# Cross attention with one head: context rows made from the turned context on TensorE instead of loaded a second time

## The chip, the cores and the metric

One program on one core of a Trainium2 chip. The metric is the device time of one launch in microseconds (us); times are medians of several runs. The profile is one further execution, recorded by the hardware profiler.

## The reference, cut to what matters

The program is a two-layer network over 32 batches of 32 query rows of width 512, with a context of 257 rows of width 512 for each batch. The change touches the first block only, a cross attention with a single head:

```python
q   = layernorm(x) @ Wq + bq                 # 32 x 32 x 512
k   = ctx @ Wk + bk                          # 32 x 257 x 512
v   = ctx @ Wv + bv
sim = einsum('bid,bjd->bij', q, k) * 512**-0.5
x   = x + einsum('bij,bjd->bid', softmax(sim), v)
```

Self-attention, a layer of experts, a second cross attention, a second self-attention and a second layer of experts follow. They are the same before and after.

## The kernel before, in words

The kernel folds the key weights into the queries, so that the scores are products of a query tile with the context itself, and it applies the value weights after the weighted sum over context rows. So each context tile is needed twice: turned (width on the partitions, `ct`, loaded from `ctxT`) for the scores, and in natural rows (context rows on the partitions, `cn`, loaded from `ctx`) for the product of the probabilities with the context. Both are loaded from HBM, all in 32-bit floats. The 257th row of each batch is held apart (`cl`, loaded from `ctxLast`).

The 1024 query rows form 8 tiles of 128 rows (`NT`), and a tile spans 4 batches (`SEQ`). For one tile the loads are 4 pieces of `ctxT` with 514 KB, 4 pieces of `ctx` with 512 KB, and one of 8 KB for the last rows. `ct`, `cn` and the small tiles exist twice, picked by `u`, the tile's parity.

The function is `cross_one_head` (L313). Two blocks prepare it: the first (L363) folds the weights and loads tile 0, the second (L513) makes the queries and loads tile 1. The third block (L567) is the stage of this text. Each engine has a program of its own, in the order in which it is written, and the engines are tied by counting semaphores. What TensorE does for a tile `n`:

- `scores` (L699 to L707): the query tile with `ct`, 16 products in 32 instructions, 257 columns each, into bank `u`.
- `turn_p` (L709): three transposes of the probabilities into bank `2 + u`.
- `p_ctx` (L717): the last row and then `cn`, into bank `4 + u`.
- `turn_a` (L734): four transposes of the weighted sum into bank 6.
- `values` (L742): 12 products with the value weights, through the helper `mm3` (L128 to L130), into bank 7.

Before its loop TensorE does `scores` of tiles 0 and 1, `turn_p` and `p_ctx` of tile 0. The loop has three turns of two steps each, so six steps; step `n` (1 to 6) is

```python
scores(n + 1, u, i + 1)
turn_p(n, 1 - u)
turn_a(n - 1, u)
p_ctx(n, 1 - u, i + u)
values(n - 1, u)
```

and a tail finishes tiles 6 and 7. ScalarE copies the query tile (`q_tile`, L597), takes the exponentials (`exps`, L601) and copies the high part of the turned sum (`a_high`, L606). VectorE finds the maximum (`softmax_top`, L631), scales the last column (`last_p`, L640), copies the turned probabilities out (`keep_p`, L644 to L646), takes the low part (`a_low`, L650), scales the sum (`keep_a`, L656) and adds to `x` (`add`, L660, L661). The SP queue loads tile `n + 2`: the turned pieces (`load_turned`) once `scores` of tile `n` are done, the natural rows (`load_rows`) once `p_ctx` of tile `n` is done.

Of the kernel before, what the change touches and what calls it, by code (L numbers as in the profile page):

```python
# [19 lines left out]
ALU = mybir.AluOpType  # L20
# [3 lines left out]
P = 128  # L24
# [17 lines left out]
LEAD = 2  # L42
# [47 lines left out]
def build(nc, d, out):  # L90
    with ExitStack() as ctx:
# [221 lines left out]
        def cross_one_head():  # L313
# [12 lines left out]
            xn = [n_area.take(D) for _ in range(4)]  # L326
            root = n_area.take(NT)
            s_ctxT = [[sem(f"xa_ctxT{u}{j}") for j in range(SEQ)] for u in range(2)]
            s_ctx = [[sem(f"xa_ctx{u}{j}") for j in range(SEQ)] for u in range(2)]
            s_cl = [sem(f"xa_last_rows{u}") for u in range(2)]  # L330
            s_sc, s_pv = sem("xa_scores"), sem("xa_pv")
            s_x, s_id, s_b, s_wq, s_wk, s_wv = (
# [11 lines left out]
                for j in range(SEQ):  # L344
                    eng.dma_start(ct[u][j], d["ctxT"][SEQ * n + j]).then_inc(s_ctxT[u][j], 16)

            def load_rows(eng, n, u):
                eng.dma_start(cl[u][0:SEQ, :], d["ctxLast"][bass.ds(SEQ * n, SEQ), :]).then_inc(s_cl[u], 16)
                for j in range(SEQ):
                    eng.dma_start(cn[u][j], d["ctx"][SEQ * n + j, 0:2 * P, :]  # L350
                                  .rearrange("(k p) e -> p k e", p=P)).then_inc(s_ctx[u][j], 16)

            jobs = [(h, c) for h in range(NHALF) for c in range(DC)]
            L, MB = 4, 4
# [4 lines left out]
            with nc.sbuf_tensor("ra_fold", [P, R_FOLD], F32R) as ra2:  # L359
# [3 lines left out]
                with nc.Block() as block:  # L363
                    @block.sync
                    def _(eng):
                        eng.dma_start(staging[0], columns(d["L0_xattn_WqT"])).then_inc(s_wq, 16)
                        eng.dma_start(staging[1], columns(d["L0_xattn_WkT"])).then_inc(s_wk, 16)
                        eng.dma_start(x[:], d["x"].rearrange("(t p) d -> p t d", p=P)).then_inc(s_x, 16)
                        eng.dma_start(staging[2], columns(d["L0_xattn_Wv"])).then_inc(s_wv, 16)
                        load_turned(eng, 0, 0)  # L370
                        eng.wait_ge(s_ql, 1)
                        eng.wait_ge(s_kl, 1)
                        load_rows(eng, 0, 0)
                        eng.wait_ge(s_x, 16)
                        eng.wait_ge(s_b, 48)

# [132 lines left out]
            with nc.sbuf_tensor("fa_cross", [P, F_CROSS], F32) as fa2:  # L509
# [3 lines left out]
                with nc.Block() as block:  # L513
                    @block.sync
                    def _(eng):
                        load_turned(eng, 1, 1)
                        load_rows(eng, 1, 1)

                    @block.vector
                    def _(eng):  # L520
                        links = Links(eng, s_links1)
                        eng.wait_ge(s_tk, 1)
                        links.link(dve.reduce_sum(through_k, banks[:, MB + 3, 0:2 * DC].rearrange("p (c k) -> p c k", k=2), AX_X))
                        for j, (h, c) in enumerate(jobs):
                            eng.wait_ge(s_mm, j + 1)
                            dve.tensor_scalar(qp[:, c, h * HALF:(h + 1) * HALF], banks[:, MB + j % 4, :], through_k[:, c:c + 1],
                                              None, ALU.add).then_inc(s_out, 1)
                            if j == 0:
                                eng.wait_ge(s_urk, 1)
                            links.link(dve.scalar_tensor_tensor(away, x[:, j, :], moments[:, j, 0:1], u_row, ALU.subtract,  # L530
                                                                ALU.mult))
                            links.link(dve.reduce_sum(shift[:, j:j + 1], away, AX_X))
                        links.link(dve.tensor_tensor(shift, shift, rstd[:], ALU.mult))
                        dve.tensor_scalar(shift, shift, both[:, 0:1], None, ALU.add)


                    @block.tensor
                    def _(eng):
                        for j, (h, c) in enumerate(jobs):
                            cols, tok = slice(c * P, (c + 1) * P), slice(h * HALF, (h + 1) * HALF)  # L540
                            if c == 0:
# [18 lines left out]
                a = [f.take(D) for _ in range(2)]  # L560
                mx, top, bias, rs, rinv = (f.take(2) for _ in range(5))
                s_passed, s_own, s_last = (sem(f"xa_{n}") for n in ("passed", "own", "p_last"))
                (s_qg, s_bias, s_exp, s_tp, s_pt, s_a, s_at, s_ah, s_al, s_o, s_xa, s_links) = (
                    sem(f"xa_{n}") for n in ("q_tile", "bias", "exp", "p_turned", "p_kept", "a_kept",
                                             "a_turned", "a_high", "a_low", "out", "x_added", "links"))

                with nc.Block() as block:  # L567
                    @block.sync
                    def _(eng):
                        gain_loads(eng)  # L570
                        with eng.Fori(0, NT // 2 - 1) as i:
                            for u in range(2):
                                n = 2 * i + u

                                eng.wait_ge(s_sc, SEQ * n + 3 * SEQ)
                                load_turned(eng, n + 2, u)

                                eng.wait_ge(s_pv, SEQ * n + 2 * SEQ)
                                load_rows(eng, n + 2, u)

                    @block.gpsimd
                    def _(eng):
# [10 lines left out]
                    def _(eng):  # L593
# [10 lines left out]
                        def a_high(n, u):  # L604
                            eng.wait_ge(s_at, n + 1)
                            act.activation(at[u][0], chunks(banks[:, 6, :]), ACT.Copy).then_inc(s_ah, 1)  # L606

                        eng.sem_inc(s_exp, LEAD)
                        q_tile(0, 0)
                        q_tile(1, 1)  # L610
                        exps(0, 0)
                        exps(1, 1)
                        with act.Fori(0, NT // 2 - 1) as i:
                            for u in range(2):
                                q_tile(2 * i + u + 2, u)
                                exps(2 * i + u + 2, u)
                                a_high(2 * i + u, u)
                        a_high(NT - 2, 0)
                        a_high(NT - 1, 1)

                    @block.vector
                    def _(eng):
# [19 lines left out]
                        def keep_p(n, u):  # L642
                            eng.wait_ge(s_tp, n + 1)
                            dve.reciprocal(rinv[:, u:u + 1], rs[:, u:u + 1])  # L644
                            dve.tensor_copy(pt[u][:, 0:2, :], banks[:, 2 + u, 0:2 * P].rearrange("p (k t) -> p k t", k=2))
                            dve.tensor_copy(pt[u][0:SEQ, 2, :], banks[0:SEQ, 2 + u, 2 * P:3 * P]).then_inc(s_pt, 1)  # L646

                        def a_low(n, u):
                            eng.wait_ge(s_ah, n + 1)
# [3 lines left out]
                        def keep_a(n, u):  # L653

                            eng.wait_ge(s_pv, SEQ * n + 2 * SEQ)
                            dve.tensor_scalar(a[u], banks[:, 4 + u, :], rinv[:, u:u + 1], None, ALU.mult).then_inc(s_a, 1)  # L656

                        def add(n, u):
                            eng.wait_ge(s_o, n + 1)
# [32 lines left out]
                    def _(eng):  # L692
# [16 lines left out]
                        def turn_p(n, u):  # L709
                            eng.wait_ge(s_last, n + 1)  # L710

                            eng.wait_ge(s_pt, n + 1)
                            for k in range(2):
                                pe.transpose(banks[:, 2 + u, k * P:(k + 1) * P], pr[u][:, k * P:(k + 1) * P], ident[:])
                            pe.transpose(banks[0:SEQ, 2 + u, 2 * P:3 * P], last[u], ident[:]).then_inc(s_tp, 1)

                        def p_ctx(n, u, i):  # L717
                            eng.wait_ge(s_pt, n + 1 + LEAD)

                            eng.wait_ge(s_a, n + 1)  # L720

                            eng.wait_ge(s_cl[u], 16 * i + 16)
                            for j in range(SEQ):
                                eng.wait_ge(s_ctx[u][j], 16 * i + 16)
                            pe.matmul(banks[:, 4 + u, :], pt[u][0:SEQ, 2, :], cl[u][0:SEQ, :], start=True, stop=False)
                            for k in range(2):
                                for j in range(SEQ):
                                    ins = pe.matmul(banks[NQ * j:NQ * j + NQ, 4 + u, :],
                                                    pt[u][:, k, NQ * j:NQ * j + NQ], cn[u][j][:, k, :],
                                                    start=False, stop=k == 1)  # L730
                                    if k == 1:
# [17 lines left out]
                            ins.then_inc(s_o, 1)  # L749

                        scores(0, 0, 0)
                        scores(1, 1, 0)
                        turn_p(0, 0)
                        p_ctx(0, 0, 0)
                        with pe.Fori(0, NT // 2 - 1) as i:
                            for u in range(2):
                                n = 2 * i + u + 1
                                scores(n + 1, u, i + 1)
                                turn_p(n, 1 - u)
                                turn_a(n - 1, u)  # L760
                                p_ctx(n, 1 - u, i + u)
                                values(n - 1, u)
                        turn_p(NT - 1, 1)
                        turn_a(NT - 2, 0)
# [1561 lines left out]
def layouts(i):  # L2326
# [4 lines left out]
    def units(up1, up2, down):  # L2331
# [8 lines left out]
    ctx = i["ctx_1024"]  # L2340
    a = {
        "x": i["x"].reshape(T, D),
        "ctx": ctx,
        "ctxT": t(ctx).reshape(B, DC, P, S).transpose(0, 2, 1, 3),
        "ctxLast": ctx[:, S - 1, :],
        "ctxLastT": ctx[:, S - 1, :].T.reshape(DC, P, B).transpose(1, 0, 2),
# [40 lines left out]
```

## Time and profile before

| | us |
|---|---|
| median of 3 timed runs | 2224.11 (2219.28 to 2225.76) |
| span of the profiled execution, first to last instruction | 2252.5 |
| the stage of this text in it (third block) | 71.8 to 171.7 |
| its six loop steps | 83.9 to 152.4 |

The profiled execution has no other time than its span: what lies around the first and the last instruction isn't given for it. The median belongs to runs without the profiler. Times within the profile count from the span's start. PE is TensorE, PEld its weight loads, DVE is VectorE, ACT ScalarE, SP the queue that issues the loads; PEclk is the granted TensorE clock as a share of its full 2.4 GHz, so that 0.50 is 1.2 GHz.

### The profile page before, as it was taken

The numbers are of one execution on the slowest core, as the hardware profiler recorded it, in microseconds if no ns is written. First come the engines' busy times: TensorE is split into PE (matmuls) and PEld (weight loads), VectorE is DVE, ScalarE is ACT, GpSimd is POOL, SyncE is SP. The second block draws the span as 40 slices with busy tenths as digits, with TensorE's granted clock in tenths as the row PEclk, the third lists the DMA queues.
The fourth block names the chain that finished last, engine by engine and source line by source line (L and its number), as shares of the span: only waits on it lengthen the run. The fifth ranks groups of instructions, "written<-read, shape, count | busy, mean of one in ns | idle before, by whom it ended". The sixth has DMA issues, their size and how long they took to land. (4 is left out here: it accounts for less than half of the span.)

```text
span 2252.5 us, 44598 instructions
## 1 busy us (share of the span) xinstructions
PE 1805.6 (80%) x15646; PEld 1506.8 (67%) x15646; DVE 911.5 (40%) x2100; ACT 615.9 (27%) x1360; POOL 794.1 (35%) x540
## 2 busy tenths in 40 slices
PE   6776898735888884289999999968772799999993
PEld 5445676524777773278888888856552688888883
DVE  5445434463333331623333333335455433333333
ACT  2112433412222220223333333334343211111110
POOL 0004331124468305223333333313103299766302
PEclk8997999867999996699999999976796899999997
DMA  6562010175556325211111111010007355443203
GB/s 247 220 240 80 20 57 1 41 302 211 167 194 210 116 71 154 91 42 39 29 37 37 28 37 28 20 43 6 25 1 287 144 179 180 147 141 124 70 20 122
DMA packets 97195, 237.09 MB, mean 105 GB/s; under 512 B 9712, under 2 KB 26736, under 8 KB 97040
## 3 DMA queue, kind: packets, MB, share of 16 engines
q1 hardware_dynamic: 68768, 172.84, 22.1%
q10 hardware_dynamic: 20592, 36.98, 5.0%
q0 software_dynamic: 7680, 25.17, 3.3%
q8 instruction: 102, 1.67, 0.3%
q14 instruction: 53, 0.43, 0.1%
HBM read 183.58 MB, written 51.38 MB: 104 GB/s over the span
## 5 line engine op out<-in xcount | busy, mean ns | idle before, releaser
L128 PE MATMUL banks<-ra_DE 128*128 128x258 f32 (+2 forms) x912 | 321.0, 353 | 30.5 <-ACT fa_DE L2058 8.4
L128 PE MATMUL banks<-weights_F,rest_r_F 128*128 x920 | 304.5, 331 | 15.3 <-DVE rest_r_F L1752 11.2
L129 PE MATMUL banks<-ra_DE 128*128 128x258 f32 (+2 forms) x912 | 311.0, 342 | 0.0
L130 PE MATMUL banks<-ra_DE 128*128 128x258 f32 (+2 forms) x912 | 310.3, 341 | 0.0
L129 PE MATMUL banks<-weights_F,rest_r_F 128*128 x920 | 282.2, 307 | 0.0
L130 PE MATMUL banks<-weights_F,rest_r_F 128*128 x920 | 280.4, 305 | 0.0
L128 PE MATMUL banks<-weights_C,rest_r_C 128*128 (+1 forms) x486 | 172.0, 354 | 59.5 <-issue 32.5
L128 PEld LDWEIGHTS banks<-ra_DE 128*128 128x128 f32 (+1 forms) x912 | 177.1, 195 | 63.4 <-ACT fa_DE L2058 14.8
L128 PEld LDWEIGHTS banks<-weights_F,rest_r_F 128*128 128x128 f32 x920 | 174.6, 190 | 50.6 <-issue 39.4
L130 PEld LDWEIGHTS banks<-ra_DE 128*128 128x128 f32 (+1 forms) x912 | 178.0, 195 | 19.3
L129 PEld LDWEIGHTS banks<-ra_DE 128*128 128x128 f32 (+1 forms) x912 | 178.2, 196 | 16.2
L1579 POOL TENSOR_TENSOR weights_F<-rest_F,weights_F 128x1536 fp32r<-128x1536 f32 x52 | 181.9, 3498 | 4.2
L130 PEld LDWEIGHTS banks<-weights_F,rest_r_F 128*128 128x128 f32 x920 | 174.6, 190 | 6.6
L129 PEld LDWEIGHTS banks<-weights_F,rest_r_F 128*128 128x128 f32 x920 | 175.1, 190 | 1.9
L128 PEld LDWEIGHTS banks<-weights_C,rest_r_C 128*128 128x128 f32 x486 | 92.3, 190 | 90.2 <-issue 89.0
L129 PE MATMUL banks<-weights_C,rest_r_C 128*128 (+1 forms) x486 | 151.0, 311 | 0.0
L2025 POOL TENSOR_TENSOR fa_DE<-fa_DE 128x1028 f32<-128x1028 f32 x32 | 60.9, 1902 | 254.3 <-DVE fa_DE L2121 254.3
L130 PE MATMUL banks<-weights_C,rest_r_C 128*128 (+1 forms) x486 | 150.2, 309 | 0.0
L1645 ACT ACTIVATE rest_F<-banks 128x128 f32<-128x128 f32 x184 | 51.3, 279 | 343.3 <-PE banks L130 343.3
L2112 DVE TENSOR_TENSOR fa_DE<-banks,fa_DE 128x512 f32<-128x512 f32 x64 | 44.3, 692 | 231.0 <-PE banks L130 231.0
L1577 POOL CAST weights_F<-rest_F 128x1536 fp32r<-128x1536 f32 x52 | 76.4, 1469 | 103.8 <-PE banks L130 99.7
L2016 POOL TENSOR_TENSOR ra_DE<-fa_DE,ra_DE 128x1032 fp32r<-128x1032 f32 x32 | 77.4, 2420 | 89.2 <-ACT ra_DE L2050 89.2
(460 smaller groups left out, 3606.4 us busy)
## 6 DMA issues: line engine op xcount, KB each, us to landing
rest_F<-in_L_units SPq DMA_DIRECT2D x52, 768.0 KB, 4.4
rest_C<-in_L_units SPq DMA_DIRECT2D x30, 768.0 KB
fa_DE<-in_ctxT SPq DMA_DIRECT2D x32, 514.0 KB, 4.0
e_sorted<-temps_C SPq DMA_DIRECT2D x1, 12032.0 KB, 38.3
rest_C<-e_sorted ACTq DMA_DIRECT2D x47, 256.0 KB, 2.7
ea_y_scratch<-rest_C ACTq DMA_DIRECT2D x47, 256.0 KB, 2.4
tail_F<-in_L_units SPq DMA_DIRECT2D x12, 768.0 KB, 21.9
fa_AB<-in_ctxT SPq DMA_DIRECT2D x16, 514.0 KB, 9.6
```

The lines of the kernel that those rows point to most:

```text
L128: pe.matmul(psum, lh, rh, start=first, stop=False)
L129: pe.matmul(psum, lh, rl, start=False, stop=False)
L130: return pe.matmul(psum, ll, rh, start=False, stop=last)
L1577: pool.tensor_copy(hi, raw).then_inc(s_pair, 1)
L1579: pool.tensor_tensor(lo, raw, hi.bitcast(F32), ALU.subtract).then_inc(s_split, 1)
L1645: act.activation(sg[q % 2], banks[:, HB + q % 2, 0:P], ACT.Silu).then_inc(s_sg, 1)
L2016: pool.tensor_tensor(cx[u][1], stg[u], cx[u][0].bitcast(F32), ALU.subtract).then_inc(s_cl, 1)
L2025: pool.tensor_tensor(pr[u][:, :, 0:S], pr[u][:, :, 0:S], rinv[:, u, :].unsqueeze(2).to_broadcast([P, DC, S]), ALU.mult).then_inc(s_pn, 1)
L2112: dve.tensor_tensor(v[u][:, k, :], banks[:, k, :], bvb, ALU.add).then_inc(s_v, 1)
```

## The change

`ctx` is no longer an input, and `load_rows` shrinks to `load_last`, which loads only the last rows (8 KB for a tile). For every tile TensorE turns `ct` back in eight groups of four 128 x 128 transposes (`turn_rows`). A group fills one whole bank, 3 or 5 by turns, and ScalarE copies it into `cn` (`keep_rows`). So 32 transposes and 8 copies of 128 x 512 are new for a tile. Banks 3 and 5 come from `turn_p`, which now has bank 2 alone, and from `p_ctx`, which has bank 4 alone.

The groups are spread over the step: two at its head, two behind `turn_p`, two behind `turn_a`, two behind `p_ctx`. On ScalarE the first four copies stand before the tile's `exps`, and the last four behind `a_high`. A group waits until ScalarE has copied the group two places earlier; `p_ctx` waits for all eight copies of its tile. SP may load over `ct` only when all eight groups of that tile are turned.

```diff
@@ SP
-            def load_rows(eng, n, u):
+            def load_last(eng, n, u):
                 eng.dma_start(cl[u][0:SEQ, :], d["ctxLast"][bass.ds(SEQ * n, SEQ), :]).then_inc(s_cl[u], 16)
-                for j in range(SEQ):
-                    eng.dma_start(cn[u][j], d["ctx"][SEQ * n + j, 0:2 * P, :]
-                                  .rearrange("(k p) e -> p k e", p=P)).then_inc(s_ctx[u][j], 16)
...
                                 eng.wait_ge(s_sc, SEQ * n + 3 * SEQ)
+                                eng.wait_ge(s_nt, ROWS * n + ROWS)
                                 load_turned(eng, n + 2, u)
@@ ScalarE
+                        def keep_rows(n, u, which):
+                            for g in which:
+                                eng.wait_ge(s_nt, ROWS * n + (g + 1))
+                                if g == 0 and not (isinstance(n, int) and n < 2):
+                                    eng.wait_ge(s_pv, SEQ * n)
+                                act.activation(cn[u][g // 2][:, g % 2, :], banks[:, (3, 5)[g % 2], :],
+                                               ACT.Copy).then_inc(s_nk, 1)
...
                         q_tile(0, 0)
                         q_tile(1, 1)
+                        keep_rows(0, 0, range(0, 4))
                         exps(0, 0)
+                        keep_rows(0, 0, range(4, ROWS))
                         exps(1, 1)
+                        keep_rows(1, 1, range(ROWS))
...
+                                q_tile(n, u)
+                                keep_rows(n, u, range(0, 4))
+                                exps(n, u)
                                 a_high(2 * i + u, u)
+                                keep_rows(n, u, range(4, ROWS))
@@ TensorE
+                        def turn_rows(n, u, which, loaded=None):
+                            for g in which:
+                                j, k = divmod(g, 2)
+                                if loaded is not None and k == 0:
+                                    eng.wait_ge(s_ctxT[u][j], 16 * loaded + 16)
+                                if not (isinstance(n, int) and ROWS * n + g < 2):
+                                    eng.wait_ge(s_nk, ROWS * n + (g - 1))
+                                for c in range(DC):
+                                    ins = pe.transpose(banks[:, (3, 5)[k], c * P:(c + 1) * P],
+                                                       ct[u][j][:, c, k * P:(k + 1) * P], ident[:])
+                                ins.then_inc(s_nt, 1)
...
                         scores(0, 0, 0)
+                        turn_rows(0, 0, range(0, 4))
                         scores(1, 1, 0)
+                        turn_rows(0, 0, range(4, ROWS))
                         turn_p(0, 0)
+                        turn_rows(1, 1, range(0, 2))
                         p_ctx(0, 0, 0)
+                        turn_rows(1, 1, range(2, ROWS))
                         with pe.Fori(0, NT // 2 - 1) as i:
                             for u in range(2):
                                 n = 2 * i + u + 1
+                                turn_rows(n + 1, u, range(0, 2), i + 1)
                                 scores(n + 1, u, i + 1)
                                 turn_p(n, 1 - u)
+                                turn_rows(n + 1, u, range(2, 4))
                                 turn_a(n - 1, u)
+                                turn_rows(n + 1, u, range(4, 6))
                                 p_ctx(n, 1 - u, i + u)
+                                turn_rows(n + 1, u, range(6, ROWS))
                                 values(n - 1, u)
```

## Rows read from the trace of the kernel before

**Rows 1.** Page, part 1: engine, busy us, share of the span, instructions.

```profile
PE 1805.6 (80%) x15646; PEld 1506.8 (67%) x15646; DVE 911.5 (40%) x2100; ACT 615.9 (27%) x1360; POOL 794.1 (35%) x540
```

**Rows 2.** Windows view, the stage's three parts. Columns stand in its header line.

```profile
core 0: us, PE busy (x) PEld busy (x) DVE busy (x) ACT busy (x) POOL busy (x), PEclk, DMA share, GB/s
71.80:83.90 12.10, 8.90 (x85) 3.65 (x85) 2.91 (x12) 4.09 (x8) 0.39 (x2) 0.86 0.64 217
83.90:152.40 68.50, 54.88 (x414) 29.37 (x415) 28.96 (x70) 9.03 (x23) 0.00 (x0) 0.95 0.89 339
152.40:171.70 19.30, 11.94 (x54) 7.33 (x52) 8.74 (x15) 1.19 (x2) 0.00 (x0) 0.91 0.00 0
```

**Rows 3.** Timeline of one tile step: start, length, engine, line, operation.

```profile
109.94 1.95 PE L704 MATMUL banks<-fa_AB 128*32 128x257 f32 x32
...
111.81 0.44 PE L714 MATMUL banks<-ident,fa_AB 128*128 128x128 f32 x2
...
112.19 0.60 PE L739 MATMUL banks<-ident,fa_AB 128*128 128x128 f32 x4
...
114.30 1.09 PE L725 MATMUL banks<-fa_AB 4*128 4x512 f32 x2 [1.51 <-DVE fa_AB L646]
...
117.18 0.50 PE L128 MATMUL banks<-ra_cross 128*128 128x512 f32 x1
...
120.75 1.95 PE L704 MATMUL banks<-fa_cross,fa_AB 128*32 128x257 f32 x32 [0.56 <-DMA fa_cross<-in_ctxT]
```

**Rows 4.** Windows view, a steady stretch of the loop; same columns.

```profile
110.00:120.00 10.00, 8.49 (x70) 4.48 (x69) 5.03 (x12) 1.57 (x4) 0.00 (x0) 1.00 1.04 404
```

**Rows 5.** Waits of TensorE, 83.9 to 152.4: us, times, longest.

```profile
PE banks L704 <- DMA fa_cross<-in_ctxT: 6.9, 3, 4.9
PE banks L725 <- DVE fa_AB L646: 5.4, 5, 1.5
PE banks L704 <- DMA fa_AB<-in_ctxT: 1.8, 2, 1.2
```

**Rows 6.** Timeline, sixteen transposes back to back, and four with the copy behind them.

```profile
29.54 1.91 PE L489 MATMUL banks<-ident,na_AB 128*128 128x128 f32 x16
...
161.49 0.60 PE L739 MATMUL banks<-ident,fa_AB 128*128 128x128 f32 x4
...
162.12 0.60 ACT L606 ACTIVATE ra_cross<-banks 128x512 fp32r<-128x512 f32 x1 [8.13 <-PE banks L739]
```

**Rows 7.** Timeline of the stage's first part.

```profile
73.01 1.28 ACT L601 ACT_TABLE_LOAD   x1
...
75.28 2.61 PE L704 MATMUL banks<-fa_cross,fa_AB 128*32 128x257 f32 x32
...
76.56 0.48 ACT L601 ACTIVATE fa_AB<-banks,fa_AB 128x257 f32<-128x257 f32 x1 [2.26 <-DVE fa_AB L634]
...
79.54 0.23 DVE L640 TENSOR_SCALAR fa_AB<-fa_AB 128x4 f32<-128x4 f32 x1 [0.50 <-ACT fa_AB L601]
...
80.08 0.27 DVE L646 COPY fa_AB<-banks 4x128 f32<-4x128 f32 x1
...
80.41 1.12 PE L725 MATMUL banks<-fa_AB 4*128 4x512 f32 x2 [0.76 <-DVE fa_AB L646]
...
83.94 1.95 PE L704 MATMUL banks<-fa_AB 128*32 128x257 f32 x32 [0.55 <-DMA fa_AB<-in_ctxT]
```

**Rows 8.** Windows view: clock after a wait, and over transposes.

```profile
94.00:98.70 4.70, 0.00 (x0) 0.02 (x1) 1.95 (x3) 0.00 (x0) 0.00 (x0) 0.84 1.03 404
98.70:102.00 3.30, 3.29 (x32) 1.57 (x32) 0.00 (x0) 0.00 (x0) 0.00 (x0) 0.50 1.06 412
30.00:34.00 4.00, 4.00 (x39) 4.00 (x38) 4.00 (x8) 2.30 (x5) 0.00 (x0) 1.00 0.02 4
34.00:36.00 2.00, 2.00 (x19) 2.00 (x19) 1.37 (x3) 0.50 (x2) 0.00 (x0) 0.93 0.00 0
36.00:38.00 2.00, 1.66 (x8) 1.25 (x6) 1.81 (x3) 1.49 (x4) 0.00 (x0) 0.50 0.00 0
```

More of the change, by code:

```diff
@@ L328, in cross_one_head @@
             s_ctxT = [[sem(f"xa_ctxT{u}{j}") for j in range(SEQ)] for u in range(2)]
-            s_ctx = [[sem(f"xa_ctx{u}{j}") for j in range(SEQ)] for u in range(2)]
             s_cl = [sem(f"xa_last_rows{u}") for u in range(2)]
@@ L370, in _ @@
                         load_turned(eng, 0, 0)
-                        eng.wait_ge(s_ql, 1)
-                        eng.wait_ge(s_kl, 1)
-                        load_rows(eng, 0, 0)
+                        load_last(eng, 0, 0)
                         eng.wait_ge(s_x, 16)
@@ L516, in _ @@
                         load_turned(eng, 1, 1)
-                        load_rows(eng, 1, 1)
+                        load_last(eng, 1, 1)
                     @block.vector
@@ L562, in cross_one_head @@
                 s_passed, s_own, s_last = (sem(f"xa_{n}") for n in ("passed", "own", "p_last"))
+                s_nt, s_nk = sem("xa_rows_turned"), sem("xa_rows_kept")
+                ROWS = 2 * SEQ
                 (s_qg, s_bias, s_exp, s_tp, s_pt, s_a, s_at, s_ah, s_al, s_o, s_xa, s_links) = (
@@ L575, in _ @@
                                 eng.wait_ge(s_sc, SEQ * n + 3 * SEQ)
+                                eng.wait_ge(s_nt, ROWS * n + ROWS)
                                 load_turned(eng, n + 2, u)
                                 eng.wait_ge(s_pv, SEQ * n + 2 * SEQ)
-                                load_rows(eng, n + 2, u)
+                                load_last(eng, n + 2, u)
                     @block.gpsimd
@@ L610, in _ @@
                         q_tile(1, 1)
+                        keep_rows(0, 0, range(0, 4))
                         exps(0, 0)
+                        keep_rows(0, 0, range(4, ROWS))
                         exps(1, 1)
+                        keep_rows(1, 1, range(ROWS))
                         with act.Fori(0, NT // 2 - 1) as i:
                             for u in range(2):
-                                q_tile(2 * i + u + 2, u)
-                                exps(2 * i + u + 2, u)
+                                n = 2 * i + u + 2
+                                q_tile(n, u)
+                                keep_rows(n, u, range(0, 4))
+                                exps(n, u)
                                 a_high(2 * i + u, u)
+                                keep_rows(n, u, range(4, ROWS))
                         a_high(NT - 2, 0)
@@ L644, in keep_p @@
                             dve.reciprocal(rinv[:, u:u + 1], rs[:, u:u + 1])
-                            dve.tensor_copy(pt[u][:, 0:2, :], banks[:, 2 + u, 0:2 * P].rearrange("p (k t) -> p k t", k=2))
-                            dve.tensor_copy(pt[u][0:SEQ, 2, :], banks[0:SEQ, 2 + u, 2 * P:3 * P]).then_inc(s_pt, 1)
+                            dve.tensor_copy(pt[u][:, 0:2, :], banks[:, 2, 0:2 * P].rearrange("p (k t) -> p k t", k=2))
+                            dve.tensor_copy(pt[u][0:SEQ, 2, :], banks[0:SEQ, 2, 2 * P:3 * P]).then_inc(s_pt, 1)
                         def a_low(n, u):
@@ L655, in keep_a @@
                             eng.wait_ge(s_pv, SEQ * n + 2 * SEQ)
-                            dve.tensor_scalar(a[u], banks[:, 4 + u, :], rinv[:, u:u + 1], None, ALU.mult).then_inc(s_a, 1)
+                            dve.tensor_scalar(a[u], banks[:, 4, :], rinv[:, u:u + 1], None, ALU.mult).then_inc(s_a, 1)
                         def add(n, u):
@@ L710, in turn_p @@
                             eng.wait_ge(s_last, n + 1)
-                            eng.wait_ge(s_pt, n + 1)
+                            eng.wait_ge(s_pt, n + LEAD)
                             for k in range(2):
-                                pe.transpose(banks[:, 2 + u, k * P:(k + 1) * P], pr[u][:, k * P:(k + 1) * P], ident[:])
-                            pe.transpose(banks[0:SEQ, 2 + u, 2 * P:3 * P], last[u], ident[:]).then_inc(s_tp, 1)
+                                pe.transpose(banks[:, 2, k * P:(k + 1) * P], pr[u][:, k * P:(k + 1) * P], ident[:])
@@ new lines, in turn_p @@
+                            pe.transpose(banks[0:SEQ, 2, 2 * P:3 * P], last[u], ident[:]).then_inc(s_tp, 1)
+                        def turn_rows(n, u, which, loaded=None):
[9 more added lines that the diff above has]
+                                ins.then_inc(s_nt, 1)
@@ L717, in p_ctx @@
                         def p_ctx(n, u, i):
                             eng.wait_ge(s_pt, n + 1 + LEAD)
-                            eng.wait_ge(s_a, n + 1)
+                            eng.wait_ge(s_a, n + LEAD)
                             eng.wait_ge(s_cl[u], 16 * i + 16)
-                            for j in range(SEQ):
-                                eng.wait_ge(s_ctx[u][j], 16 * i + 16)
-                            pe.matmul(banks[:, 4 + u, :], pt[u][0:SEQ, 2, :], cl[u][0:SEQ, :], start=True, stop=False)
+                            eng.wait_ge(s_nk, ROWS * n + ROWS)
@@ L726, in p_ctx @@
+                            pe.matmul(banks[:, 4, :], pt[u][0:SEQ, 2, :], cl[u][0:SEQ, :], start=True, stop=False)
                             for k in range(2):
                                 for j in range(SEQ):
-                                    ins = pe.matmul(banks[NQ * j:NQ * j + NQ, 4 + u, :],
+                                    ins = pe.matmul(banks[NQ * j:NQ * j + NQ, 4, :],
                                                     pt[u][:, k, NQ * j:NQ * j + NQ], cn[u][j][:, k, :],
@@ L2342, in layouts @@
         "x": i["x"].reshape(T, D),
-        "ctx": ctx,
         "ctxT": t(ctx).reshape(B, DC, P, S).transpose(0, 2, 1, 3),
```

## The prediction

> **What bounds the kernel now.** I read the page first: TensorE is the busiest engine [rows 1], but that is an average over stages. The windows view of the stage [rows 2] shows something else there. In the six loop steps TensorE is busy 54.9 of 68.5 us while the transfer engines are at 0.89, and the clock is at full speed for most of it (0.95). In a steady stretch the transfers are saturated (share 1.04, 404 GB/s) [rows 4]. A tile needs 4 x 514 + 4 x 512 + 8 = 4112 KB, 4.21 MB, which takes 10.4 us at 404 GB/s. The step in the timeline takes 120.75 - 109.94 = 10.81 us [rows 3], so the old loop is bound by its transfers, but not by much. The waits of TensorE in the loop agree: 6.9 + 1.8 us for turned context, of which one wait is 4.9, and 5.4 us for the copy of the turned probabilities [rows 5]. Together that is 14.1 us of idle in six steps, so some 2.3 a step. That is all that work put on TensorE can hide in.
>
> **What one step costs TensorE without waits.** From `scores` to `scores` 10.81 us, less the two waits of 1.51 and 0.56, is 8.74 us [rows 3]. Two ends in it are drains that a following instruction would hide: the four transposes of `turn_a` are listed with 0.60 us and cost 0.44 in a stream (below), and the last product of `values` has a like tail. So 8.5 to 8.74.
>
> **Removed.** Half the bytes: a tile falls to 2.06 MB and 4 turned pieces, 2.11 MB, or 5.2 us at 404 GB/s. SP issues four transfers fewer for each tile, and nobody waited for its issuing. In the loop the 14.1 us of waits go, and a low clock: after the 4.9 us wait the clock was at 0.50, and 32 instructions of `scores` needed 3.29 us and more where they take 1.87 at full speed [rows 3, 8]: at least 1.4 us, and with the last of them and the transposes behind at half speed I estimate 2.7. What is late next is TensorE's own stream.
>
> **Added on TensorE, loop.** 32 transposes a tile. Sixteen in a row took 1.91 us with the last one's drain, start to start 0.11 [rows 6]; so 32 x 0.11 = 3.5 us. Nothing hides them: TensorE does one thing at a time, and the idle places are gone with the waits. A step becomes 8.5 to 8.74 + 3.5 = 12.0 to 12.3 us; I take 12.2. Six steps: 73.2 us, against 68.5 with all old waits in it. So +4.7 us.
>
> **Does anything else set the step?** ScalarE gets eight copies of 0.60 us [rows 6], 4.8 us beside its own two copies of that width and `exps` (0.48 with 0.19 for the sum's read [rows 7]), some 1.9: 6.7 of 12.2. A group's copy begins about 0.64 us after the group's first transpose and ends 0.60 later, and the handing back to TensorE costs 0.06 (from the end of L646 at 80.35 to L725 at 80.41) [rows 7], so a bank comes round in 1.30 us. In the loop the groups stand in pairs with other work between, so a bank is back before the pair after needs it; the tightest is the third pair, behind `turn_a` only. With scores ending at 2.8 us of the step, the second pair is copied by about 4.9, and the third pair's second group wants to start at 5.0. It fits, just. `exps` comes 0.8 us later than before, behind two copies, but its result (`last_p`) is wanted by TensorE a step later. `p_ctx`, which waited 1.51 us for VectorE's copy, now finds it done behind four groups (1.8 us). `turn_p` on one bank waits for the copy of the tile before, a step old. On SP, `load_turned` of tile `n + 2` waits for the last group of tile `n`, at 9.2 us of a step. The piece is wanted a whole step and 3 us later, 15 us, for a transfer of 5.2 us and some start-up; hidden. Behind it in the SP queue is only the load of the last rows.
>
> **Added on TensorE, before the loop.** This is the part where I expect most. Here two tiles' groups, 64 transposes, meet `exps` and the copies on one ScalarE. The old loop began at 83.94, of which 0.55 was a transfer [rows 7]. The new order, by the same durations:
> - `scores` of tile 0 free TensorE at 75.28 as before [rows 7]. Four groups follow on two banks: two pairs, one every 1.30 us, the second pair's own 0.9 behind: free at 77.6. `scores` of tile 1 then, to 79.5.
> - ScalarE ends the fourth copy at 78.4, then loads its table (1.28 us [rows 7], until now hidden behind `scores`), to 79.7, and `exps` of tile 0 (0.67 with its read of the sum) to 80.35.
> - Groups 5 and 6 end at 80.4, but group 7 waits for the copy of group 5, which stands behind `exps`: 81.0; group 8 ends at 82.0. `turn_p` to 82.35, two groups of tile 1 to 83.25 (the second waits for a copy).
> - `exps` of tile 1 stands behind these copies: to 83.4. VectorE's order has `last_p` of tile 1 before `keep_p` of tile 0: from L640 at 79.54 to the end of L646 at 80.35 took 0.81 us [rows 7], so with hand-offs `p_ctx` starts at 84.4 and ends at 87.3 (114.30 to 117.18, 2.88 us [rows 3]).
> - Six groups of tile 1 with nothing between, limited by the banks: three pairs at 1.30 less the last wait, 3.6 us. The loop begins at 90.8.
>
> So +6.9 us. Nothing else works in that time that could be late: tile 2 is requested at 82 and landed by about 90. The ends for this term are 64 x 0.11 less the 1.2 to 2 us of old waits there, about +5, and +9 if each hand-over takes twice what I took.
>
> **The clock.** At 30 to 34 us TensorE was busy 4.00 of 4.00 us with transposes and products of two columns, and still the clock fell, 0.93 and then 0.50 with the engine busy 1.66 of 2 us [rows 8]. So on this chip a stretch that holds nothing but transposes can lose the clock. The Trainium skill (TensorE: Matmul & The Clock Gate, Part 4: PE-mode transpose) says that the full clock does not engage for transposes; the trace agrees for this stretch. Taken for every step of the loop, the rule would give the clock rival's time below; taken by the old loop's rows, the sum's. In the loop the longest stretch of transposes alone is 0.4 + 0.9 + 0.4 + 0.9 = 2.6 us; before the change there was a stretch as long at 111.81 to 114.30, idle and transposes, and the clock stayed at 1.00 [rows 3, 4]. I expect it to stay in the loop. Before the loop there are two longer stretches (79.5 to 84.4, and 87.3 to 91.7 with the first pair of the loop). A fall costs 1.5 to 3 us (2.7 above). Taking a bit under even odds for each: +1.3 us.
>
> **Sum.** 6.9 + 4.7 + 1.3 = +12.9 us. The tail behind the loop (19.3 us, no transfers [rows 2]) is the same code and starts later. All from the profiled execution, of which only the span (2252.5) is given; that is 28 us above the median, and the difference is not in any row. I apply the difference to the median: 2224.1 + 12.9 = 2237.0 us. Its own range is 2230 to 2244.
>
> **Rivals.**
> - No change, not slower: in the timed runs the old transfers are slower than in the profile, and the old loop longer by as much. What the change gains is then the excess of old steps. To make up 12.9 us each of six steps would have had to be 2.1 us longer, 12.9 us: 4.21 MB in it is 326 GB/s. For: the mean over the loop is 339 [rows 2]. Against: this mean holds a stretch with nothing requested, and the steady rate is 404 [rows 4]. It decides from a steady rate of about 340 down (within 0.3%). It would give 2224 to 2230.
> - The banks' handshake binds in the loop too: each pair costs 1.30 instead of 0.88 us, 4 x 0.42 x 6 = +10 us more, 2247. For: the third pair fits by a tenth. Against: the other three have a microsecond to spare.
> - The clock falls in every step: 6 x 2.7 = +16, with both falls before the loop +3, 2256. For: the fall at 35 us [rows 8]. Against: the clock at 1.00 over a like stretch of old steps [rows 4].
> - Faster: a transpose in a stream of products costs half, 0.055, because the 0.11 belongs to streams of transposes alone. 32 x 6 x 0.055 = -10.6 us, and with less wait before the loop 2222. Against: in the loop three of them took 0.38 us (111.81 to 112.19), 0.13 each [rows 3].
>
> **How the numbers follow.** The forecast 0.60, no change by slower transfers 0.14, the handshake 0.11, the clock in each step 0.07, cheap transposes and other gains 0.08. About 0.3% (6.7 us) is what a measurement of this kernel tells from no change. Slower by more than that: most of the forecast (0.58), the handshake, the clock: 0.76. Within: 0.17. Faster: 0.07. The range holds the forecast, the upper part of the no-change case and the handshake: 2226 to 2249.
>
> **What would show it.** After the change: TensorE's waits for transfers in the loop gone, the step 12.0 to 12.4 us from `scores` to `scores` with the transfer rate near 175 GB/s, the loop's first step beginning 6 to 8 us later from the stage's start, and the step's groups without idle before them. Wrong would be a step under 11.3 us, idle before the groups of the third pair, or PEclk under 0.9 in the loop.

## The result, and the profile after

The changed kernel is slower by half a percent, about as much as was forecast.

| | before | after |
|---|---|---|
| median of 5 timed runs each | 2219.28 us | 2230.51 us |
| lowest to highest | 2216.99 to 2225.76 | 2227.83 to 2233.91 |
| ratio after/before | | 1.0054, 95% interval 1.0039 to 1.0068 |
| span of the profiled execution | 2252.5 | 2232.2 |

The ratio is worth 12 us of 2219. The spans of the two profiles point the other way, for a reason outside the changed stage: the profiled execution of before was 14 us ahead of after's when the first layer of experts began (first of its copies at 492.7 us, against 506.3) and 20 us behind when it ended (last addition to `x` at 923.6, against 903.5). So it lost some 34 us there, in code that is the same; what slowed it is open. The stage in question can be compared in the two profiles all the same. From the first product of tile 0 to the first transposes of the layer norm behind the stage, before needs 72.53 to 176.48 = 103.95 us, after 72.98 to 191.09 = 118.11 us, which is 14.2 us more.

The windows view of after, with four stretches ahead of the loop, the loop, three stretches of the tail, and the columns of [rows 2]:

```profile
76.00:79.00 3.00, 2.75 (x24) 2.01 (x24) 0.80 (x3) 1.56 (x3) 0.00 (x0) 0.87 0.00 0
79.00:83.00 4.00, 3.75 (x47) 2.50 (x48) 0.94 (x4) 3.71 (x8) 0.00 (x0) 1.00 0.00 0
83.00:88.00 5.00, 4.37 (x32) 1.86 (x30) 0.80 (x4) 2.34 (x6) 0.00 (x0) 1.00 0.68 210
88.00:92.00 4.00, 3.55 (x28) 2.53 (x24) 0.75 (x1) 2.62 (x5) 0.00 (x0) 1.00 0.73 267
92.20:165.40 73.20, 73.20 (x607) 48.23 (x607) 28.68 (x69) 34.51 (x73) 0.00 (x0) 1.00 0.40 145
165.40:168.00 2.60, 0.93 (x8) 0.66 (x6) 2.02 (x4) 0.60 (x1) 0.00 (x0) 1.00 0.00 0
168.00:171.00 3.00, 2.32 (x6) 0.51 (x10) 1.23 (x5) 0.00 (x0) 0.00 (x0) 0.65 0.00 0
171.00:174.00 3.00, 3.00 (x16) 0.39 (x8) 0.00 (x0) 0.00 (x0) 0.00 (x0) 0.50 0.00 0
```

The row 92.20:165.40 answers to [rows 2]: in its six steps TensorE is now busy 73.20 of 73.20 us, at the full clock, while the transfers fell from 0.89 to 0.40 and from 339 to 145 GB/s (175 from 104 to 141 us, as forecast; nothing is left to load in the last steps). The bound has passed from the transfers to TensorE, and the new one is longer: 73.2 us against 68.5.

One step on TensorE's timeline, to be read beside [rows 3] (L717 is `scores`, L727 and L728 `turn_p`, L764 `turn_a`, L750 the first product of `p_ctx`, L739 the new groups):

```profile
116.67 1.03 PE L739 MATMUL banks<-ident,fa_AB 128*128 128x128 f32 x8
117.64 1.95 PE L717 MATMUL banks<-fa_AB 128*32 128x257 f32 x32
119.52 0.44 PE L727 MATMUL banks<-ident,fa_AB 128*128 128x128 f32 x2
...
119.90 1.04 PE L739 MATMUL banks<-ident,fa_AB 128*128 128x128 f32 x8
120.77 0.60 PE L764 MATMUL banks<-ident,fa_AB 128*128 128x128 f32 x4
121.21 1.12 PE L739 MATMUL banks<-ident,fa_AB 128*128 128x128 f32 x8
122.26 1.12 PE L750 MATMUL banks<-fa_AB 4*128 4x512 f32 x2
...
125.17 1.09 PE L739 MATMUL banks<-ident,fa_AB 128*128 128x128 f32 x8
...
128.86 1.03 PE L739 MATMUL banks<-ident,fa_cross 128*128 128x128 f32 x8
129.83 1.95 PE L717 MATMUL banks<-fa_cross,fa_AB 128*32 128x257 f32 x32
```

From 117.64 to 129.83 is 12.19 us, and no row carries a wait. The two waits of [rows 3] (1.51 for VectorE's copy, 0.56 for a transfer) are gone; in their place stand four times two groups.

The part before the loop, to be read beside [rows 7]:

```profile
72.98 3.36 PE L717 MATMUL banks<-fa_AB 128*32 128x257 f32 x32 [3.83 <-ACT fa_AB L594]
...
76.27 1.31 PE L739 MATMUL banks<-ident,fa_AB 128*128 128x128 f32 x8
...
77.83 1.15 PE L739 MATMUL banks<-ident,fa_AB 128*128 128x128 f32 x8 [0.25 <-ACT fa_AB L612]
...
78.91 1.95 PE L717 MATMUL banks<-fa_cross,fa_AB 128*32 128x257 f32 x32
79.64 1.28 ACT L598 ACT_TABLE_LOAD   x1
...
84.93 0.27 DVE L659 COPY fa_AB<-banks 4x128 f32<-4x128 f32 x1
...
85.26 1.12 PE L750 MATMUL banks<-fa_AB 4*128 4x512 f32 x2 [0.64 <-DVE fa_AB L659]
...
89.51 1.14 PE L739 MATMUL banks<-ident,fa_cross 128*128 128x128 f32 x8 [0.25 <-ACT fa_cross L612]
...
90.86 1.15 PE L739 MATMUL banks<-ident,fa_cross 128*128 128x128 f32 x8 [0.20 <-ACT fa_cross L612]
...
92.20 1.15 PE L739 MATMUL banks<-ident,fa_AB 128*128 128x128 f32 x8 [0.20 <-ACT fa_cross L612]
```

The loop begins at 92.20 where it began at 83.94, and 7.8 us later when counted from the start of tile 0's scores. The last pairs of groups of tile 1 and the first pair of tile 2 follow each other by 1.34 us (89.51, 90.86, 92.20) where two groups need 0.88 of TensorE. That is the hand-over of two banks between TensorE and ScalarE.

### The profile page after: what moved, and what is told of

It is laid out like the page before. It is cut to its first block and busy times, and to the rows that moved or that the text cites. A ratio compares the mean times of both kernels' runs of the same rounds, so it can differ in the third digit from the quotient of the medians.

```text
span 2232.2 us, 45202 instructions
## 1 busy us (share of the span) xinstructions
PE 1830.8 (82%) x15902; PEld 1529.9 (69%) x15902; DVE 912.3 (41%) x2100; ACT 649.1 (29%) x1424; POOL 799.1 (36%) x540
## 5 line engine op out<-in xcount | busy, mean ns | idle before, releaser
L128 PE MATMUL banks<-weights_F,rest_r_F 128*128 x920 | 304.5, 331 | 15.6 <-DVE rest_r_F L1785 11.4
```

Source lines behind the costliest of these rows:

```text
L128: pe.matmul(psum, lh, rh, start=first, stop=False)
```

## The experiments

Each is compared with the kernel before, timed beside it on the same chip. h1, h2, c1 and c2 ran on another chip than the kernels e and f, so between kernels the ratios compare, not the times. There are 12 timed executions of each, 7 of f1, 5 of after and e4, and one of c1 and c2. "Stage" is the time from tile 0's scores to the next layer norm's transposes in the one profile of each kernel, "loop" its six steps.

| kernel | ratio to before (95%) | stage | loop | clock in the loop |
|---|---|---|---|---|
| before | 1 | 104.0 | 68.5 | 0.95 |
| after | 1.0054 (1.0039 to 1.0068) | 118.1 | 73.2 | 1.00 |
| e1 rows from the first tiles | 0.9989 (0.9969 to 1.0009) | 104.5 | 65.5 | 0.91 |
| e2 first two tiles turned | 1.0024 (1.0006 to 1.0042) | 115.2 | 66.8 | 0.95 |
| e3 first two tiles loaded | 1.0012 (0.9994 to 1.0030) | 109.7 | 73.4 | 1.00 |
| e4 turned twice | 1.0147 (1.0114 to 1.0181) | 138.6 | 93.7 | 1.00 |
| h1 two batches turned, in the wait | 0.9985 (0.9971 to 0.9998) | 100.2 | 64.8 | 1.00 |
| h2 one batch turned | 0.9977 (0.9966 to 0.9989) | 101.9 | 62.9 | 1.00 |
| f1 as e1, waits filled | 0.9955 (0.9938 to 0.9973) | 96.5 | 59.9 | 1.00 |
| f2 all loaded, new banks | 0.9995 (0.9983 to 1.0008) | 104.6 | 68.0 | 0.95 |
| f3 as f2, waits filled | 0.9997 (0.9981 to 1.0012) | 108.7 | 70.3 | 0.93 |

**The two halves of the change.** e2 keeps the new order before the loop and loads the rows of tiles 2 to 7; e3 is its counterpart.

```diff
 e2, in the loop of SP
+                                load_rows(eng, n + 2, u)
 e2, in the loops of TensorE and ScalarE
-   turn_rows(...) and keep_rows(...), all
 e3, blocks 1 and 2, SP
+                        load_rows(eng, 0, 0)        # and load_rows(eng, 1, 1)
 e3, before the loops of TensorE and ScalarE
-   turn_rows(...) and keep_rows(...), all
```

> The change in the part before the loop alone: tiles 0 and 1 are turned in the new order, tiles 2 to 7 load their natural rows as before. Theory (the two parts add): the loop begins 7 to 8 us later than before, the loop itself stays near 68 us, perhaps up to 3 us shorter because its requests start better spread; together 5 to 8 us over the kernel before (ratio 1.002 to 1.0035). Rival (the loss is all in the loop, and the later start is absorbed by loads that get ahead): within 2 us of before.

> The change in the loop alone: tiles 0 and 1 load their natural rows as before, tiles 2 to 7 are turned. Theory: the loop begins at its old place, steps are 12.2 us as in the changed kernel, loop 73 us; 4 to 5 us over the kernel before (ratio 1.002), 7 to 8 under the changed one. Rival (bank hand-over between TensorE and ScalarE sets the step too): the same here, so it is not told apart; rival (the loss is all before the loop): within 1 us of before.

Measured: e2 +5.3 us (0.24%), e3 +2.7 us (0.12%, an interval that reaches to no change). Against the changed kernel e3 is 9.3 us faster and e2 6.7. In the profiles e3's loop takes 73.4 us, 4.9 more than before's, and begins 10.6 us behind tile 0's scores against 11.4, since its first groups stand where TensorE waited for a transfer. e2's loop begins 10.0 us later than before's and not 7.8: its first sixteen transposes ran mostly at half clock (3.31 us, against 1.91 in [rows 6]), and TensorE waited 1.5 us at the loop's start for ScalarE's next query tile, which is queued behind the copies. That loop is 1.7 us shorter than before's; I put this down to requests that are better spread, which no run isolates. e2's profiled execution took 2228.8 us, 5 above its median, so its stage of 115.2 us is a long one.

The timed sum, +8 us, is below the change's own +12, but the intervals reach that far. What follows: the profiles show both halves longer, the part before the loop by 7.8 to 10.0 us and the loop of turned tiles by 4.7 to 4.9. The timed runs alone show only that the new order before the loop costs something (e2); they don't tell e3 from no change, and they don't rank the halves.

**What a transpose costs.** e4 does each group in the loop twice over.

```diff
-                                for c in range(DC):
+                                for c in (range(DC) if isinstance(n, int) else [*range(DC)] * 2):
                                     ins = pe.transpose(...)
```

> In the loop each group of four transposes is done twice over into the same bank (same result, same copies, same transfers): 32 transposes more for each of six tiles. Theory (nothing hides a transpose in the loop, 0.11 us each): 6 x 32 x 0.11 = 21 us more than the changed kernel, so 33 over the kernel before (ratio 1.015), step 15.7 us, and the clock in the loop at 1.00. Rival (ScalarE's copies and the banks set the step, transposes partly hidden behind them): under 12 us more. Rival (transposes hold the clock down): PEclk under 0.9 in the loop and more than 25 us.

Measured: +32.6 us by the ratio, against the changed kernel's +12: 20.6 us for 192 transposes, 0.107 each; the loop's profile gives 93.7 - 73.2 = 20.5. A transpose in a full step costs its whole length, and the rival with ScalarE's copies as the limit (under 12 us more) is out. Between `scores` and `p_ctx` there are now 4.4 us of nothing but transposes, and still the clock stayed:

```profile
110.00:126.00 16.00, 16.00 (x145) 11.77 (x142) 5.51 (x13) 6.58 (x13) 0.00 (x0) 1.00 0.39 145
126.00:142.00 16.00, 16.00 (x149) 11.78 (x145) 5.40 (x13) 6.30 (x13) 0.00 (x0) 1.00 0.39 143
...
157.00:173.00 16.00, 16.00 (x149) 11.78 (x145) 5.53 (x13) 6.50 (x13) 0.00 (x0) 1.00 0.14 58
```

That speaks against my reading of [rows 8].

**What the halved transfers give.** e1 leaves both out.

```diff
@@ SP, in the loop
-                                load_rows(eng, n + 2, u)
@@ TensorE, p_ctx
-                                eng.wait_ge(s_ctx[u][j], 16 * i + 16)
+                                eng.wait_ge(s_ctx[u][j], 16)
```

> Neither turned nor loaded: the natural rows of tiles 0 and 1 are loaded as in the kernel before, and the six loop steps go on using them (so tiles 2 to 7 take wrong rows; all other work and the new bank use are kept). This is the gain of the halved transfers alone. Theory (TensorE is the new bound, transfers were the old one): a step is TensorE's 8.74 us plus the wait for VectorE's copy of 1.5, so 10.2 us instead of 11.4 on average; loop 61 instead of 68.5 us, 7 us less than the kernel before (ratio about 0.997), transfer waits of TensorE near zero. Rival (the old transfers were not the bound, only the first long wait was): no more than 5 us less, steps still above 10.8.

Measured: 2.4 us under before, a third of what I expected, with an interval that holds no change. In time this is the rival's "no more than 5 us less", but not in its steps, which it wanted above 10.8 us: TensorE waits for no transfer in the loop any more, only the wait for VectorE is left, and the undisturbed steps take 9.8 to 10.2 us. The steps were not even: their `scores` begin at 96.78, 106.71, 120.11, 131.67 us, so 9.9, 13.4 and 11.6 us. The windows of the long one, and of a stretch ahead of the loop, from the same profile:

```profile
80.00:86.00 6.00, 5.24 (x19) 1.29 (x22) 0.80 (x4) 0.47 (x1) 0.00 (x0) 0.56 0.49 188
...
106.00:111.00 5.00, 3.56 (x43) 1.97 (x41) 3.57 (x10) 0.82 (x3) 0.00 (x0) 1.00 0.96 367
111.00:115.00 4.00, 3.92 (x14) 0.89 (x18) 0.70 (x2) 0.75 (x2) 0.00 (x0) 0.56 0.12 50
115.00:118.00 3.00, 3.00 (x12) 1.48 (x5) 0.75 (x1) 0.00 (x0) 0.00 (x0) 0.50 0.01 3
```

TensorE is busy 3.00 of 3.00 us and the clock is at half: it fell at the end of a wait, after transposes and 1.5 us of idle. Ahead of the loop it was low as well, so that the loop began 13.3 us behind tile 0's scores and the stage is no shorter than before's. So the saved transfer time was given back to the clock. Whether the idle or the transposes did it is for the next runs.

**Which work holds the clock.** c1 and c2 are the changed kernel with 80 instructions put in just before the loop.

```diff
+                        for _ in range(80):
+                            pe.transpose(banks[:, 7, 0:P], bv[:, 0:P], ident[:])                            # c1
+                            pe.matmul(banks[:, 7, 0:2], ones[:], ones[:, 0:2], start=True, stop=True)      # c2
```

> The changed kernel with 80 more transposes of one 128 x 128 block into bank 7, back to back just before the loop, nine us of nothing else. Theory A (transposes count as activity for the clock; the fall at 35 us in the kernel before came from the two-column products): PEclk 1.00 all through, 80 x 0.11 = 8.8 us. Theory B (transposes don't count, as I took it in the prediction): the clock falls to 0.50 within this stretch, and a transpose then takes 0.21 us.

> The same place with 80 products of 128 x 128 weights with two columns instead, back to back. Theory A: the clock falls to 0.50 in or right behind this stretch although TensorE is busy all through. Theory B: it falls too (no useful difference); if it stays at 1.00, theory A's reading of the fall at 35 us is wrong.

The timeline row of the 80 and the windows over them, first c1, then c2:

```profile
90.79 8.90 PE L785 MATMUL banks<-ident,fa_AB 128*128 128x128 f32 x80
```

```profile
94.00:96.00 2.00, 2.00 (x21) 2.00 (x19) 0.00 (x0) 0.00 (x0) 0.00 (x0) 1.00 1.02 393
96.00:98.00 2.00, 2.00 (x21) 2.00 (x20) 0.00 (x0) 0.00 (x0) 0.00 (x0) 1.00 0.90 360
98.00:100.00 2.00, 2.00 (x21) 2.00 (x20) 0.00 (x0) 0.00 (x0) 0.00 (x0) 1.00 0.01 4
```

```profile
90.55 12.63 PE L785 MATMUL banks<-ones 128*128 128x2 f32 x80
```

```profile
94.00:96.00 2.00, 2.00 (x18) 2.00 (x18) 0.00 (x0) 0.00 (x0) 0.00 (x0) 0.90 0.98 389
96.00:98.00 2.00, 2.00 (x11) 2.00 (x11) 0.00 (x0) 0.00 (x0) 0.00 (x0) 0.50 0.81 331
98.00:100.00 2.00, 2.00 (x11) 2.00 (x11) 0.00 (x0) 0.00 (x0) 0.00 (x0) 0.50 0.03 12
```

In both PE and PEld are busy 2.00 of 2.00 us. Transposes alone keep 1.00 for nine us; two-column products lose the clock and keep it lost, to 0.50. So the busy share in the profile doesn't tell the two apart. I put the fall at 35 us in [rows 8] down to the 32 two-column products of L504, which ran from 31.21 to 34.94 us, between the transposes there. Each kernel ran once (2240.1 us and 2247.0, where the changed kernel's median is 2230.5), but the stretches are long and the answer isn't near a bound. The Trainium skill (TensorE: Matmul & The Clock Gate, Part 4: PE-mode transpose) has it that the full clock doesn't engage for transposes; the measurement decides, and here they held it.

Whether transposes alone can raise a clock that is low is not shown. In e2 it rose in the middle of sixteen transposes (0.50 from 77 to 79 us, 0.99 from 79 to 80), but 3.6 us of scores at half clock stand just ahead of them.

**Filling the waits.** f1 is e1 with eight useless transposes in each step's wait; f2 is the kernel before with the new bank use alone, f3 the same with the filling.

```diff
                                 turn_a(n - 1, u)
+                                for _ in range(8):
+                                    pe.transpose(banks[:, 3, 0:P], bv[:, 0:P], ident[:])
                                 p_ctx(n, 1 - u, i + u)
```

> As the kernel that neither turns nor loads (wrong rows for tiles 2 to 7), with eight transposes of a constant block into the free bank 3 put into each step's wait between turn_a and p_ctx: 0.88 us of useless work in a wait of 1.2 to 1.5. Theory (that kernel gained 2.4 us instead of 7 because the idle in each step let the clock fall twice in its loop; transposes count as activity): no step at half clock, steps 9.9 to 10.2 us, loop 60 to 61.5 us against 65.3 without the filling, 6 to 8 us under the kernel before (ratio 0.9965 to 0.9973). Rival (the falls came by chance or from the transfers): loop 65 as before, or longer by 5 us for the filling.

> The kernel before with nothing but the new use of the banks (turn_p in bank 2 alone, p_ctx in bank 4 alone, banks 3 and 5 unused). Both theories: the same time as before within 0.1%, since each bank's last reader is done a step earlier; it is the base for the next kernel.

> The same with the eight filling transposes in each step's wait. Theory: nothing lost, since they stand in idle time, and what the clock sometimes loses in the short waits is saved: 0 to 3 us under the kernel before (the 4.9 us transfer wait stays and goes on costing its fall). Rival (a transpose costs its 0.11 us wherever it stands): 5 us over.

f1 does all that e1 does and 48 transposes more, and is faster: 10 us under before (6 to 14 by its interval) instead of 2.4, with its loop at 59.9 us:

```profile
82.50:144.00 61.50, 57.36 (x465) 32.63 (x462) 28.93 (x70) 8.90 (x23) 0.00 (x0) 1.00 0.48 175
```

The intervals of e1 and f1 overlap only from 0.9969 to 0.9973, and that f1 owes its gain to the clock rests on one profile of each. f2 shows that the bank use costs nothing (0.9995). f3 excludes the rival's 5 us more. Its 0.7 us under before lie within the 0 to 3 that I expected, but aren't told from nothing: its loop waits for transfers, and it is there that the clock is lost (waits of 4.7 and 2.3 us). In these two pairs the filling of short waits paid only where the long ones were gone.

**A mix.** h1 and h2 load the rows of tiles 0 and 1, and turn only as much as TensorE's old wait can take; the rest is loaded.

```diff
+                TURNED = 2                      # h1; 1 in h2
+                ROWS = 2 * TURNED
@@ SP
+                                load_rows(eng, n + 2, u, range(TURNED, SEQ))
@@ TensorE, the step of h1 (h2: one turn_rows of two groups, behind turn_a)
                                 scores(n + 1, u, i + 1)
                                 turn_p(n, 1 - u)
+                                turn_rows(n + 1, u, range(0, 2))
                                 turn_a(n - 1, u)
+                                turn_rows(n + 1, u, range(2, 4))
                                 p_ctx(n, 1 - u, i + u)
                                 values(n - 1, u)
```

> A mix: tiles 0 and 1 load their natural rows as before; of tiles 2 to 7 batches 0 and 1 are turned (four groups, two behind turn_p and two behind turn_a, all ahead of p_ctx) and batches 2 and 3 load their rows. Transfers for a tile 3.15 MB, 7.8 us at 404 GB/s. Theory (old step = transfers and idle at about the same length; a group placed in the wait for VectorE's copy costs nothing, and full TensorE keeps its clock): step 10.3 us, loop 62 us against 68.5, PEclk 1.00 in the loop; 5 to 7 us under the kernel before (ratio 0.997 to 0.998). Rival (a transpose costs its 0.11 us wherever it stands): step 10.2 + 1.8 = 12.0, 3 to 4 us over before.

> As the mix, with batch 0 alone turned (two groups between turn_a and p_ctx); transfers 3.63 MB, 9.0 us. Theory: the wait for VectorE's copy is shortened by the groups and not filled, step 10.2 us, loop 61 to 62 us; 5 to 7 us under before unless the idle left (0.6 us a step) costs the clock in a step or two, which is 2 to 3 us each. Rival (transposes cost 0.11 us wherever): 11.1 us a step, within 2 us of before.

Both are faster than both kernels: h1 by 3.3 us and h2 by 5.1 us against before, so h2 by some 17 against the change (0.9977 against 1.0054). h1 misses the 5 to 7 us that I expected, and its interval ends at 0.9998, so its lead over before is barely told from none; h2's is clear. The two aren't told apart. TensorE's waits in h1 and h2, from just ahead of the loop to its end (L728 and L727 are `scores`, L762 is `p_ctx`; us, times, longest):

```profile
PE banks L728 <- DMA fa_cross<-in_ctxT: 1.6, 1, 1.6
PE banks L728 <- DMA fa_AB<-in_ctxT: 0.6, 1, 0.6
```

```profile
PE banks L727 <- DMA fa_cross<-in_ctxT: 3.1, 2, 2.1
PE banks L762 <- DVE fa_AB L668: 1.9, 3, 0.7
PE banks L727 <- DMA fa_AB<-in_ctxT: 1.5, 1, 1.5
```

h1's later steps are 10.49 us (105.81 to 116.30), 16 transposes included, where e1's undisturbed ones are 9.8 to 10.2 without any: 0.3 to 0.7 us for 1.8 us of work. Its first step still takes 12.4 us, which keeps its loop at 64.8 instead of the 62 expected. h2's loop (62.9) is nearer to its 61 to 62; transfers still cost it 3.1 us of waits, and VectorE's copy 1.9. The last row of each view is the wait for tile 2 at the loop's head. That h2's stage is longer than h1's (101.9 against 100.2), though its loop is shorter, comes from the tail, 26.9 us against 24.1. The rival, that a transpose costs 0.11 us wherever it stands, falls here.

## Why the prediction was right

Forecast 2237.0 from a base of 2224.1, which is +12.9 us; measured +11.2 by the medians and +12 by the ratio. Term by term, from the profile:

- **The bound.** Right that transfers and TensorE were near each other, with 2.3 us of idle a step as all there was to win. f1 shows what taking all natural rows off the transfers can win when the clock is held too: 10 us, 6 to 14 by its interval.
- **The loop, +4.7 us.** Forecast 12.2 us a step and 73.2 in all; profile 12.19 and 73.2. Sixteen transposes of 1.91 us [rows 6] were the right row, and e4 confirms the price at 0.107 us.
- **Nothing else sets the step.** Right: TensorE has no wait in a step, the third pair starts at 121.21, 0.44 us behind the start of `turn_a`, as soon as its four transposes are through. SP's later request was hidden as worked out.
- **Before the loop, +6.9 us.** Measured +7.8. The chain came as described (table load in the open, `exps` behind copies, `last_p` of tile 1 before `keep_p` of tile 0: L659 ends at 85.20 and `p_ctx` starts 0.06 later). Two sizes were a little short. `p_ctx` began 12.28 us behind tile 0's scores, where the forecast comes to 11.87, since the low clock at the stage's start lasted longer: tile 0's scores took 3.29 us to the next instruction against 2.75 before (72.53 to 75.28). The three pairs of tile 1 took 4.03 us (88.17 to 92.20) instead of 3.5, since hand-overs were 1.34 instead of 1.30 and the last one's wait came ahead of the loop.
- **The clock, +1.3 us.** This term failed. I laid the fall in [rows 8] to the transposes, though 3.7 us of two-column products stand in the same stretch, and expected falls in the two stretches of transposes before the loop; the windows from 79 on show 1.00, and c1 shows that transposes can hold it. A fall came in the tail instead, 168 to 174 us at 0.65 and 0.50: from 165.40 to the next layer norm 25.7 us, against 24.05 before, 1.6 us that I had at nothing. It follows an idle wait of 2.36 us that the kernel before has too. These are that wait in before, and a later stretch of its tail:

```profile
155.71 1.12 PE L725 MATMUL banks<-fa_AB 4*128 4x512 f32 x2 [2.35 <-DVE fa_AB L646]
...
162.00:168.00 6.00, 3.50 (x11) 2.71 (x11) 2.36 (x4) 0.60 (x1) 0.00 (x0) 0.79 0.00 0
```

Before held its clock behind the wait (`p_ctx`'s first product took 1.12 us, against 1.88 in after) and lost it some ten us later. The tail takes 24.1 us in before, h1, f1 and c2, 25.4 to 25.8 in after, e1, e3, e4, f2 and c1, and 26.9 in e2, f3 and h2. f2, which turns no rows at all, has after's tail, and h1 and c2, which do, have before's. So it goes with where the falls land and not with the turned rows; what decides that isn't shown. That the size of the whole term was near was luck.
- **Rivals.** The handshake in the loop and a clock that falls in each step are excluded by the loop's row (73.20 busy, 1.00). Cheap transposes are excluded by e4. That old transfers were slower in timed runs isn't seen: f2, which is the old loop, has 68.0 us in an execution of 2217.1 us, within the range of the timed runs of before.

The profile's stage difference, 14.2 us, is 7.8 + 4.7 + 1.6; the timed one is 11 to 12. Falls of the clock of 2 to 3 us each, which come and go from one profile to the next, are as large as what is left.

## What to carry to other kernels

Bytes can be traded for TensorE work only up to TensorE's idle time: here that was 2.3 us in a mean step of 11.4, and 3.5 us of transposes were put in. The same trade with a quarter of the rows, placed in a wait that TensorE has anyway, wins, and with half of them it wins barely; and whatever could be loaded in a time when nobody waits (here tiles 0 and 1) should not be computed.

## What the runs showed of the hardware that was not expected

- Transposes of 128 x 128 in 32 bits, back to back, held the full clock for 8.9 us; 80 products with two columns, begun at 90.55 us with TensorE just as busy in the profile, brought it to 0.90 from 94 to 96 us and to 0.50 from 96 on, and took 12.63 us. At the full clock it would be about 9, an estimate from the 3.73 us of the 32 at L504.
- Work put into a wait made a kernel faster: with 48 transposes more the loop went from 65.5 to 59.9 us, 9.8 to 10.2 us a step without exception, with the clock at 1.00 all through (e1 and f1, one profile each; by the timed runs 0.9989 and 0.9955).
- The clock can fall in a step with only 1.5 us of idle beside its transposes (e1, at 111 us), and needn't in a like one (the kernel before, at 114 us [rows 3, 4]).
